# Two reorderings at the start of a four-layer conditioned kernel: the modulation's products behind the first generation pass on TensorE, and the query weights' split behind the adapter's first activation

## The reference, cut to what matters

```python
# L0: an adapter whose weights are generated for each sequence
dWd = ((h_lang @ Wdd.T + bdd) * 0.1).reshape(B, 128, 256)     # Wdd is (32768, 64)
dWu = ((h_lang @ Wdu.T + bdu) * 0.1).reshape(B, 256, 128)
down = relu(einsum('bld,bnd->bln', x, Wd + dWd) + bd)
x = x + einsum('bln,bdn->bld', down, Wu + dWu) + bu
# L1: layer norm, weight, bias, plus tanh(cond @ lin_w.T + lin_b), weight, bias
# L2: a transformer block, modulated by six vectors for each sequence
t = silu(t_embd @ W_t1.T + b_t1) @ W_t2.T + b_t2
cond = silu(t + c_embd) @ W_c.T + b_c
g1, b1, g2, b2, a1, a2 = split(cond, 6)
h = layernorm(x) * g1 + b1;  q, k, v = split(h @ W_qkv.T + b_qkv, 3)
x = x + (softmax(q k / 4) v @ W_o.T + b_o) * a1               # 16 heads of 16
x = x + (gelu((layernorm(x) * g2 + b2) @ W_f1.T + b_f1) @ W_f2.T + b_f2) * a2
# L3: rms norm, gated feed-forward, ternary down weights, quantised activations
```

## Time and profile before

| | us |
|---|---|
| median of three executions | 933.14 |
| range | 932.55 to 935.09 |
| the profiled execution's own time | 935.74 |
| its span on the core | 933.9 |
| TensorE busy in the span | 843.1 (90%) |
| VectorE busy | 565.4 (61%) |
| ScalarE busy | 510.9 (55%) |
| GpSimd busy | 231.2 (25%) |

### The profile page before, as it was taken

How to read it: one execution, slowest core, us unless ns; L and a number is a source line. 1 busy time by engine, 2 the same in 40 slices (tenths; PEclk the granted TensorE clock), 3 DMA queues, 4 the chain that set the end, 5 groups by cost and what they waited for, 6 DMA issues and landing times.

```text
span 933.9 us, 15916 instructions
## 1 busy us (share of the span) xinstructions
PE 843.1 (90%) x5852; PEld 633.5 (68%) x5852; DVE 565.4 (61%) x1063; ACT 510.9 (55%) x796; POOL 231.2 (25%) x333
## 2 busy tenths in 40 slices
PE   6642577999999999999999999999999999999977
PEld 4101355687777778787878787878777777776665
DVE  1212586575757667575858585858485867656424
ACT  1101444565565657574748575656666574756542
POOL 1001204150405041323232231405050514130310
PEclk9855777999999999999999999999999999999998
DMA  9997643423161433324151515151424132320000
GB/s 344 365 366 252 248 138 124 148 80 122 62 203 38 135 97 114 120 78 156 47 187 47 188 47 188 46 173 61 154 76 142 65 127 80 104 80 25 24 12 12
DMA packets 58477, 118.48 MB, mean 127 GB/s; under 512 B 6336, under 2 KB 15936, under 8 KB 55696
## 3 DMA queue, kind: packets, MB, share of 16 engines
q1 hardware_dynamic: 58400, 117.48, 36.6%
HBM read 82.77 MB, written 34.16 MB: 125 GB/s over the span
## 4 chain that ended last, share of the span: by engine, by line
PE 74%; issue 9%; DMA 7%; DVE 4%; ACT 2%; SPq 2%; POOL 2%; POOLq 0%; DVEq 0%; ACTq 0%
PE bank L486 30%; PE bank L692 11%; PE pair_s L653 6%; PE pair_s L618 5%; PE pair_t L639 5%; PE pair_t L486 4%; DMA hyp<-in_hyper 3%; PE bank L737 3%; PE bank L664 3%; PE bank L567 2%; PE bank L729 1%; PE bank L561 1%; DVE oq L1145 1%; DMA wc<-in_cols 1%; PE bank L574 1%
## 5 line engine op out<-in xcount | busy, mean ns | idle before, releaser
L851 ACT ACTIVATE Pr<-pair_t 128x1024 f32<-128x1024 f32 x128 | 131.3, 1026 | 125.2 <-PE pair_t L639 121.5
L1121 DVE TENSOR_REDUCE nmax<-pair_s 128x4 f32<-128x1024 f32 x128 | 155.8, 1217 | 34.5 <-PE pair_s L618 33.9
L692 PE MATMUL bank<-wf,G 128*128 128x256 f32 x512 | 123.0, 387 | 0.1
L486 PE MATMUL bank<-wup_hi,hD_hi 128*128 128x512 f32 x256 | 109.4, 427 | 4.8 <-POOL hD_lo L1316 4.1
L1344 POOL TENSOR_TENSOR x<-x,xcr 128x512 f32<-128x512 f32 x16 | 20.5, 1281 | 358.1 <-DVE x L1179 358.1
L692 PEld LDWEIGHTS bank<-wf,G 128*128 128x128 f32 x512 | 93.3, 190 | 15.5 <-issue 0.2
L486 PE MATMUL bank<-wup_lo,hD_hi 128*128 128x512 f32 x256 | 102.0, 398 | 0.0
L486 PE MATMUL bank<-wup_hi,hD_lo 128*128 128x512 f32 x256 | 101.9, 398 | 0.0
L618 PE MATMUL pair_s<-Kp,Qp 64*128 64x256 f32 x512 | 66.1, 337 | 21.7 <-DVE nmax L1121 13.0
L895 ACT ACTIVATE gl<-bank,rsD 128x512 f32<-128x512 f32 x64 | 44.1, 689 | 63.6 <-PE bank L486 63.4
L1189 DVE SCALAR_TENSOR_TENSOR hd<-bank,rsD,gl 128x512 f32<-128x512 f32 x64 | 47.9, 748 | 46.2 <-PE bank L486 34.7
(11 more groups left out here) (177 smaller groups left out, 1879.5 us busy)
## 6 DMA issues: line engine op xcount, KB each, us to landing
hyp<-in_hyper SPq DMA_DIRECT2D x16, 1024.0 KB, 10.2
Qp<-qk_scratch SPq DMA_DIRECT2D x64, 256.0 KB, 3.7
Kp<-qk_scratch SPq DMA_DIRECT2D x64, 256.0 KB, 3.6
qk_scratch<-q_hi SPq DMA_DIRECT2D x16, 512.0 KB, 2.8
qk_scratch<-k_hi SPq DMA_DIRECT2D x16, 512.0 KB, 4.0
tC<-rows_scratch SPq DMA_DIRECT2D x16, 384.0 KB, 3.6
cur_scratch<-gen SPq DMA_DIRECT2D x16, 256.0 KB, 10.1
xT_t<-in_xT SPq DMA_DIRECT2D x16, 256.0 KB, 4.2
```

The costliest lines, as they stand in the source:

```text
L486: mm = pe.matmul(dst, l, r, start=first and i == 0, stop=last and i == 2)
L692: mm = pe.matmul(bank[5][:, r * D:(r + 1) * D], G[:, k, r * P:(r + 1) * P], wf2[:, k, :], start=k == 0, stop=k == FT - 1)
L851: act.activation(Pr[:, p % 4, :, :].rearrange("p a n -> p (a n)"), pair_t[:, :, :].rearrange("p a n -> p (a n)"), ACT.Exp, scale=DH ** -0. ...
L1121: dve.tensor_reduce(nmax[:, n % 2, :, p % GP, :], pair_s[:, :, :].rearrange("p a (r n) -> p a r n", r=RT), AX.X, ALU.max, negate=True).the ...
```

## The change

The change alters only orders. Three places:

1. On TensorE, the products of chunks (0, 2) and (0, 3) move ahead of the modulation's products. The wait for `wc` and everything behind it now stands after chunk (0, 3).
2. On VectorE, the copy of chunk (0, 3) moves with it, from behind the last table sum that needs TensorE to ahead of the first.
3. In turn 0, `W.qkv` moves on ScalarE from ahead of `A.down` to behind it, and on VectorE from ahead of `A.up` to behind `A.ln`.

SP's order, ScalarE's order in the prologue and every wait's count are the same.

```diff
     "ACT": """
-        0: W.qkv A.down A.lnb A.ht A.q W.fa A.k A.v 1: A.down W.up ...
+        0: A.down W.qkv A.lnb A.ht A.q W.fa A.k A.v 1: A.down W.up ...
...
     "DVE": """
-        0: W.qkv A.up A.lna A.lng A.ln A.q A.cur A.k 1: A.up ...
+        0: A.up A.lna A.lng A.ln W.qkv A.q A.cur A.k 1: A.up ...
...
             generate(0, 1)
+            generate(0, 2)
+            generate(0, 3)
             pe.wait_ge(wc_in, 16)
             pe.wait_ge(prep, PREP.index("s2") + 1)
             for m in range(8):
...
             mm.then_inc(pre_pe, 1)
-            generate(0, 2)
             pe.wait_ge(wo_in, 16)
             pe.wait_ge(small_in, 16)
             pe.wait_ge(prep, PREP.index("mod") + 1)
             for k in range(KT):
                 mm = pe.matmul(bank[6][0:NB, 0:D], bv[:, k:k + 1].to_broadcast([P, NB]), wo[:, k, :], ...)
             mm.then_inc(pre_pe, 1)
-            generate(0, 3)
             with pe.Fori(1, NCH // 4) as i:
...
             generated(0, 1)
+            generated(0, 3)
             dve.wait_ge(pre_pe, 3)
...
             step(dve.tensor_tensor(tb[:, 7, :], bank[6][0:NB, 0:D], b_o, ALU.add))
-            generated(0, 3)
             dve.wait_ge(pre_act, 3)
```

More of the change, by code:

```diff
@@ L85 @@
     "ACT": """
-        0: W.qkv A.down A.lnb A.ht A.q W.fa A.k A.v 1: A.down W.up A.lnb A.ht B.t0 B.t1 A.q B.t2 B.t3 B.t4 A.k B.t5 A.v B.t6 B.t7 2: A.down C.lnb C.ht
+        0: A.down W.qkv A.lnb A.ht A.q W.fa A.k A.v 1: A.down W.up A.lnb A.ht B.t0 B.t1 A.q B.t2 B.t3 B.t4 A.k B.t5 A.v B.t6 B.t7 2: A.down C.lnb C.ht
         A.lnb C.f0 C.f1 A.ht C.f2 C.f3 B.t0 A.q B.t1 A.k B.t2 B.t3 B.t4 A.v B.t5 B.t6 B.t7 C.xt 3: A.down D.u0 C.lnb D.u1 C.ht D.u2 C.f0 A.lnb C.f1
@@ L90 @@
     "DVE": """
-        0: W.qkv A.up A.lna A.lng A.ln A.q A.cur A.k 1: A.up A.lna B.s0 A.lng B.s1 A.ln B.s2 B.s3 B.p0 B.m0 B.s4 B.s5 A.cur B.s6 B.s7 B.p1 W.fa B.m1
+        0: A.up A.lna A.lng A.ln W.qkv A.q A.cur A.k 1: A.up A.lna B.s0 A.lng B.s1 A.ln B.s2 B.s3 B.p0 B.m0 B.s4 B.s5 A.cur B.s6 B.s7 B.p1 W.fa B.m1
         W.up A.q A.k B.o1 W.abs B.o3 2: A.up C.proj C.ln B.s0 B.s1 A.lna A.lng B.s2 A.ln B.s3 B.p0 B.m0 B.s4 B.s5 A.cur B.s6 B.s7 B.p1 A.q A.k B.m1
```

## The result

The changed kernel takes 937.37 us (median of 20 executions, 934.12 to 939.50); the kernel before, run beside it, 934.81 us (20 executions, 932.55 to 936.12). The ratio is 1.0028 with a 95% interval of 1.0020 to 1.0037: 2.6 us slower. The forecast was 1.7 us slower, 934.8 us on the first median of 933.14, in a range of 930.0 to 938.0, with "within 0.3%" as the likeliest case. The kernel before itself came out 1.7 us higher here than in the first three executions, so the step, +2.6 us, is the figure to compare with the forecast, and not 937.37 with 934.8.

The account below looks back on a forecast made before the run. TensorE was taken to bound the kernel from turn 1, mostly transfers its first 70 us. Prologue +4.8 and relu -3.1 gave +1.7 us on the 933.14 median: 934.8 us, range 930.0 to 938.0.

Parts of the forecast that it names:

- within 0.3%: Whole kernel: the time stays within 0.3% (2.8 us) of the kernel before, chance 0.56; slower 0.28, faster 0.16.
- one rival's price: Turn 0, deviation behind `A.ln`: VectorE's low part holds GpSimd up, price 1.76 us, giving 936.5 us; chance 0.18.
- What bounds the kernel: Whole span: chain 74% TensorE, 7% DMA; transfers dominate the first 70 us, and the start's gain or loss passes on whole.
- The old hole: Prologue, 27.2 to 29.4 us: the transfer queue's hole of about 2.2 us closes with (0, 2) and (0, 3) first.
- a new one: Prologue: a hole of some 7 us opens at 33.4, as refill (2, 0) goes out at 39.4 instead of 31.74.
- Its price: Prologue, first two edits: the last chunk comes 4.8 us later, between 4.4 and 6.3 by the two clocks.
- VectorE's share: Prologue: copy of (1, 1) at about 41.1, refill (2, 2) near 42.3, covered by 3 us of queued transfers.
- The clock: TensorE, prologue: moved block stays slow at 12.46 us, line 515's loads near 333 ns; fast clock expected near 37.
- The first rival: Prologue: moved block runs at the fast clock, about 6.5 us instead of 12.46, giving 928.0 us; chance 0.10.
- The relu: Turn 0: with the split behind it, `dn` starts at 74.6 instead of 77.68, 3.1 us earlier.
- What arrives of it: Turn 0, third edit: the whole 3.1 us gain taken, bounds 1.3 and 3.1.
- unless GpSimd's preceding sum holds it: Turn 0: exception to the low part starting 0.2 us before GpSimd's sum at 85.40 - 3.1 and holding it up.

Follow-up runs that it names:

- e1: Kernel before with only chunks (0, 2) and (0, 3) ahead of the modulation's products, turn 0 as before: 939.0 us, 1.0042, 3.9 us slower.
- e2: Kernel before with only the query weights' split moved behind the relu and second statistics: 932.61 us, 0.9976, 2.2 us faster.
- e3: On e2, VectorE's low part waits for GpSimd's second deviation, TensorE's wait moved behind the transpose: 932.07 us, 0.9959 against the kernel before.
- e7: Kernel before with only chunk (0, 2) moved ahead of the modulation's products: 937.12 us, 1.0032, 3.0 us slower.
- e9: Kernel before with half of line 515's 16 modulation's products left out: 932.74 us, 0.9983, 1.6 us faster.
- e10: Kernel before, prologue as e5 but (0, 3) and (1, 0) behind the eighth of 16 products: 936.2 us, 1.0008 against before.
- e12: The kernel of e3 timed again on another chip: 930.52 us, 0.9955 against the kernel before.
- e8: Changed kernel plus the low-part and TensorE wait edits of e3: 933.95 us, 0.9996 against the kernel before.
- e4: Changed kernel with half of line 517's 16 modulation's products left out: 934.61 us, 0.9996 against the kernel before.
- e5: Kernel before, TensorE order (0, 2), line 515's 16 products, (0, 3), (1, 0), (1, 1), other modulation products: 936.33 us, 1.0020 against before.
- e11: The prologue order of e10 together with the query weights' split of e3: 932.73 us, 0.9974 against the kernel before.
- e6: The prologue order of e5 together with the query weights' split of e3: 932.77 us, 0.9966 against the kernel before.

## Why the prediction was right, and where it was lucky

The sign was right and the size near (1.7 us slower forecast, 2.6 measured). Of the steps behind it, one term was a good deal too large and one rival's price belonged in the sum, and the two offset each other.

**What bounds the kernel: right.** The chain's shares are 75% TensorE now, and the start goes through to the end: e1, e2, e3 and e7 each move the time the way their start shows, within 2 us. "Whole" was too strong. e9 moves the last chunk by 3 us and the time by 1.6, and e10 moves them by 2 us and not at all. I saw no slack behind turn 0 that could swallow a gain; the wait for a transfer near 272 us, between nothing and 2.1 us long, is such a place, and it is in the trace of before.

**The old hole: closed as forecast, a new one opened as forecast.** Line 517 starts at 23.38 (forecast 24.4), the queue is dry from 33.4 (33.4), and the refill (2, 0) goes out at 37.52 (39.4). I take off the half microsecond by which this execution is ahead: the products then start 0.5 and the refill 1.4 us earlier than forecast. The hole lasts about 5 us, not the 7 forecast.

**Its price: the mechanism right, the size too large.** The forecast was 4.8 us with bounds of 4.4 to 6.3. By timing, e1 costs 3.9 (2.3 to 5.4), which doesn't exclude 4.8, and its trace puts 1.0 us of it in turn 0. By the traces, counted from the first chunk to the last, the old order took 54.1, 55.7, 56.1 and 54.9 us (before, e2, e3, e12) and the new one 57.5, 58.8 and 58.0 (after, e1, e8): 58.1 against 55.2, a difference of 2.9. Two things were mis-sized. The block starts 0.5 us sooner than forecast, as chunk (0, 3) lands sooner; it is 0.3 shorter, as its last products already run at the fast clock; and chunk (1, 0) runs beside the two products of line 530 (in the trace of after it begins at 35.84, between them), so these and the chunk took 1.7 us behind the block (35.57 to 37.29) and not 2.4. The second chunk behind the restart then follows at 3.05 us, not 3.4. And I read the old order's prologue off one trace that was the best of four: the other three lose up to 2 us more between chunks, so there was more of the loss in the old order than I saw.

**VectorE's share: right.** The copy of (1, 1) comes at 39.2 and the refill (2, 2) goes out at 40.6, while the queue still works on (2, 0). The chain passes through these tables, but chunk (2, 2) starts at 49.03, 3.1 us behind (2, 1), in the cadence of the queue: an earlier refill would not have helped.

**The clock: right not to count on it.** The weight loads of the moved block were to show it. The block takes 7.01 us for its 32 records, as before, though TensorE had chunk (0, 3) right ahead of it and worked without a gap from 21.52. The first rival, the moved block at the fast clock, did not come about: that TensorE is busy wasn't enough here for the rise to 2.4 GHz. In the traces the fast durations came at about 35 (after) and 37.5 us (e1), once products of 256 and 512 columns had been running.

**The relu: 3.1 us earlier, as forecast.** 3.0 in the trace.

**What arrives of it: 1.5, not 3.1. This is the step that failed.** I had weighed it and given it 0.18: from the 32 short runs of line 1284, one of them beside a two-input instruction of VectorE, I concluded that VectorE is held up by GpSimd and not the reverse. Line 1284 takes 1.71 us in after, e2 and e4, beside a low part of 1.97, and 0.2 in e3, e8 and e12, where they don't overlap. The Trainium skill (SBUF — State Buffer, Who interferes with whom) says that a VectorE instruction with two inputs in SBUF and a GpSimd instruction that reads SBUF exclude each other, whichever comes first. Here the trace of after agrees with its number: the addition ends at 86.49, 0.05 us behind the low part's end at 86.44. The error was in the evidence: I took one harmless overlap of one kind as the rule for another. That overlap doesn't agree with what the Trainium skill says: in the trace of before, line 1095, a `scalar_tensor_tensor` of 0.51 us with two inputs in SBUF, began at 82.10, and line 1284 ran its 0.20 us inside it, from 82.15. The instruction now is a `tensor_tensor` of 1.76 us. Whether the kind or the length makes the difference, no run here separates. The forecast's way out, "unless GpSimd's preceding sum holds it", didn't help either. That sum (line 1309, 83.56 to 84.82) did overlap the start of the low part at 84.47, and the low part took 0.2 us more than its 1.76, yet it still came ahead of line 1284. And "once 1211" was misread from a maximum: line 1129 takes about 1.2 us three times in that trace, each time beside a long instruction of GpSimd.

**The sum.** +2.9 to +3.9 for the first two edits and -1.5 to -2.2 for the third give +0.7 to +2.4; e1 and e2 by their ratios give 3.9 - 2.2 = 1.7. Measured were 2.6 (1.9 to 3.5). The gap of 0.9 between these two is within the intervals. The forecast's +4.8 - 3.1 = +1.7 is near by the two errors' offset, and that is luck. With the hole at its 2.9 us and my own price for the port it would have been 2.9 - 3.1 + 1.8 = +1.6, nearly the same.

**The chances.** "Within 0.3%" at 0.56 holds, just: 0.28%. The 0.28 on slower was the right side to lean to.

## What to carry to other kernels

Filling a ring earlier is worth only what the consumer's next visit allows: when work is moved behind a refill to close a hole in a queue, ask at once which refill now stands behind that work, and compare its time with the stock. A single engine order can run a transfer queue dry even though the engine stood idle shortly before, here for 6.9 us. A long `tensor_tensor` on VectorE with two inputs in SBUF doesn't belong beside a short one of GpSimd that is on the path; a wait that puts it behind, and TensorE's own wait moved behind the transpose, gave 1.6 us back in the traces here and cost nothing that they show.

## What the runs showed of the hardware that I had not expected

- A transfer share near 1 isn't a full rate. In e5 the share was 0.97 at 306 GB/s, and at the usual pace 1.02 at 420. The packets of 8 KB took 393 to 458 ns each in that stretch (from the trace's packet records, means over 2 us) against 309 in the steady part; in e9, whose refills go out with 3 us of stock ahead, they took 309 throughout.
- The granted clock falls once more, late in some executions. In the trace of before TensorE runs at half the clock from 853.5 to 856.9, in that of after it doesn't:

```profile
853.50:856.90 3.40, 3.40 (x22) 1.85 (x24) 1.90 (x5) 1.60 (x3) 0.00 (x0) 0.50 0.00 0
```

```profile
853.50:856.90 3.40, 3.13 (x37) 1.78 (x33) 2.73 (x5) 2.05 (x3) 0.00 (x0) 1.00 0.00 0
```

From one square sum of stage C to the corresponding one of the next sequence (ScalarE, line 878) it takes 48.13 us across that place in before and 47.07 in after: 1.1 us for one such fall, as much as several of the differences under study. e4, e11 and e12 have one at 850 to 853 and e6 one at 272.8; after, e1, e2, e3, e5 and e7 to e10 have none there. This is part of why single spans could not be compared.
